# First stage of a four-layer graph network: node statistics ahead of the second mask tile; layer two's factor rows two sums sooner

## The reference, cut to what matters

```
h = relu(layernorm(x));  x = x + L0(h)   # project, layernorm, additive attention under adj, elu
h = relu(layernorm(x));  x = x + L1(h)   # 4-head attention under adj
h = relu(layernorm(x));  x = x + L2(h)   # relu(h W_self + mean over neighbours (h) W_neigh)
h = relu(layernorm(x));  x = x + L3(h)   # additive attention under adj
```

## Time and profile before

| what | us |
|---|---|
| median of 3 runs | 3532.34 (3532.33 to 3533.17) |
| the profiled execution | 3530.73 |
| its span (first to last instruction) | 3528.9 |
| mean granted TensorE clock of the span | 0.99 of full speed |

### The profile page before, as it was taken

The page is one execution under the profiler, slowest core; times in us unless marked ns, Lnnn a source line. Parts: engine busy times, 40 slices in busy tenths (PEclk is TensorE's granted clock), DMA queues, the critical chain, the costliest instruction groups (busy, mean ns, idle before and its releaser), DMA issues. The chain is left out here.

```text
span 3528.9 us, 58152 instructions
## 1 busy us (share of the span) xinstructions
PE 3409.4 (97%) x21140; PEld 1790.0 (51%) x21155; DVE 3066.7 (87%) x6862; ACT 1808.0 (51%) x4044; POOL 1830.4 (52%) x922
## 2 busy tenths in 40 slices
PE   6899998889999999999999999999998999899999
PEld 6799998431111111111111111111116999899999
DVE  8899997579999999999999999999977776677777
ACT  8633543766666666666666666666662554310010
POOL 7400101238888888888888888888870111000000
PEclk9999999999999999999999999999998999999999
DMA  8612121940011011101110111010003331312120
GB/s 301 220 69 91 55 91 54 291 161 10 25 30 30 8 27 30 30 6 29 30 30 5 30 30 30 6 30 30 6 7 108 120 120 73 121 67 91 55 91 25
DMA packets 78816, 234.62 MB, mean 66 GB/s; under 512 B 13504, under 2 KB 40768, under 8 KB 64448
## 3 DMA queue, kind: packets, MB, share of 16 engines
q1 hardware_dynamic: 77808, 230.56, 19.5%
q10 hardware_dynamic: 720, 0.33, 0.0%
HBM read 148.85 MB, written 81.99 MB: 65 GB/s over the span
## 5 line engine op out<-in xcount | busy, mean ns | idle before, releaser
L1828 POOL TENSOR_TENSOR a_w<-a_w,keep_mask_t 128x1024 f32<-128x1024 f32 x760 | 1608.0, 2141 | 306.1 <-ACT a_w L1813 306.1
L1813 ACT ACTIVATE a_w<-a_sc_ps 128x512 f32<-128x512 f32 x2048 | 1111.4, 595 | 705.1 <-PE a_sc_ps L1734 703.5
L1712 PE MATMUL a_o_ps<-a_w,a_v 128*33 128x512 f32 x4096 | 1079.1, 605 | 0.2
L1191 PE MATMUL g_acc<-g_hv,g_w 128*128 128x129 f32 x8192 | 923.2, 276 | 16.6 <-DVE g_w L1036 16.6
L1191 PEld LDWEIGHTS g_acc<-g_hv,g_w 128*128 128x128 f32 x8192 | 920.8, 193 | 17.9 <-ACT g_hv L1069 13.3
L1767 DVE CUSTOM_DVE_ANT_0 a_mx_ps<-a_mx_ps,a_mbias 128x512 f32<-128x512 f32 x1024 | 673.9, 718 | 39.5 <-PE a_mx_ps L1696 39.0
L1767 DVE CUSTOM_DVE_ANT_0 a_mx_ps<-a_mx_ps,em_mbias 128x512 f32<-128x512 f32 x968 | 636.5, 718 | 30.1 <-PE a_mx_ps L1696 29.8
L1734 PE MATMUL a_sc_ps<-a_qs,a_ks 97*128 97x512 f16 x2048 | 621.8, 385 | 0.5 <-ACT a_w L1813 0.2
L1780 DVE TENSOR_TENSOR a_w<-a_w,keep_mask_t 128x1024 f32<-128x1024 f32 x264 | 468.6, 1775 | 22.0 <-ACT a_w L1813 16.6
L1696 PEld LDWEIGHTS a_mx_ps<-a_ks,a_qs 32*128 32x128 f16 x1992 | 88.8, 91 | 784.9 <-DVE a_mx L1767 428.0
L1036 DVE SCALAR_TENSOR_TENSOR g_w<-f_row,keep_s,keep_mask_t 128x1024 f32<-128x1024 f32 x256 | 331.9, 1318 | 71.7 <-PE g_acc L1191 67.7
(11 more groups left out here) (313 smaller groups left out, 2383.2 us busy)
## 6 DMA issues: line engine op xcount, KB each, us to landing
p_adj_in<-in_adj SPq DMA_DIRECT2D x16, 1024.0 KB, 8.8
v<-p_v SPq DMA_DIRECT2D x32, 264.0 KB, 3.2
a_v<-v SPq DMA_DIRECT2D x16, 528.0 KB, 3.6
f_row<-u_rows SPq DMA_DIRECT2D x16, 512.0 KB, 5.9
g_x<-in_x SPq DMA_DIRECT2D x8, 1024.0 KB, 11.2
g_row<-u_rows SPq DMA_DIRECT2D x16, 512.0 KB, 8.1
x<-ho_o SPq DMA_DIRECT2D x16, 512.0 KB, 3.0
a_ks<-k_hi SPq DMA_DIRECT2D x64, 128.0 KB, 2.9
```

The source lines that it names most:

```text
L1191: mm = nc.tensor.matmul(tile(half, it), w[:, g % PB, it * P:(it + 1) * P], hv[:, k, jt, :], start=(jt == 0 and it % 3 == 0), stop=(jt == T ...
L1712: mm = nc.tensor.matmul(o_ps[2 * HD * a:2 * HD * a + HD + 1, c % 2, :], v[u][:, jt, a, :], w[:, g % PB, a, :], start=(jt == 0), stop=(jt = ...
L1813: nc.scalar.activation(w[:, g % PB, a], sc_ps[:, n % SB], ACT.Exp, scale=SCALE).then_inc(exp_done, 1)
L1828: nc.gpsimd.tensor_tensor(w[:, g % PB], w[:, g % PB], keep["mask_t"][:, jt, c * BANK:(c + 1) * BANK].unsqueeze(1).to_broadcast([P, 2, BANK ...
```

## The change

Three edits of order; no operation is added, removed or resized. In the first stage VectorE takes stats_x(b + 2) in front of mask(b, 1). In layer two's last round TensorE's tensor_rows comes after sum 7 instead of 9 and VectorE's vector_rows after sum 8 instead of 10. ScalarE's three exponentials come ahead of keep_h of the first two pieces instead of behind them.

```diff
--- before.py
+++ after.py
@@ -588,9 +588,9 @@
                 shift_of_x(b + 1)
                 if b > 0:
                     stats_h(b - 1, 1 - k)
-                mask(b, 1)
                 if b < B - 2:
                     stats_x(b + 2, k)
+                mask(b, 1)
                 if b > 0:
                     scores(b - 1, 1 - k)
 
@@ -2160,7 +2160,7 @@
                             fs.vector_diagonal(nc, dve, keep)
                         elif it == 5:
                             fs.vector_exponents(nc, dve, keep)
-                        elif it == 10:
+                        elif it == 8:
                             fs.vector_rows(nc, dve)
                 residual(b, k, 3)
                 stats3(b)
@@ -2269,10 +2269,11 @@
                     norm3(b - 1, 1 - k)
                     for q in range(CH):
                         keep_hT3(b - 1, q)
+                if last(b):
+                    fs.scalar(nc, act, keep)
+                if follows:
                     keep_h(b - 1, 0)
                     keep_h(b - 1, 1)
-                if last(b):
-                    fs.scalar(nc, act, keep)
                 for n in range(CH):
                     if more:
                         norm2(b + 1, 1 - k, n)
@@ -2383,7 +2384,7 @@
                         elif it == 4:
                             pe.wait_ge(consts_ready, 4)
                             fs.tensor_spread(nc, pe, keep)
-                        elif it == 9:
+                        elif it == 7:
                             fs.tensor_rows(nc, pe, keep)
                     if it in (4, 5) and follows:
                         turn3(b - 1, 2 * (it - 4))
```

## The result

The changed kernel takes 3543.7 us (median of 8 runs, 3540.39 to 3545.46), the kernel before 3532.9 us (8 runs beside it, 3529.83 to 3534.38). The ratio is 1.003, 95% interval 1.0021 to 1.0039: slower, by 0.21% to 0.39%. The forecast was 3536.6, with a range up to 3541.5.

A forecast was written before the change was run, and what follows sets the result against it. TensorE, busy 97% of the span, was taken as the bound, with VectorE, ScalarE and DMA nearly full in the first stage. First-stage reorder +4.3 us plus layer-two edits 0, on 3532.3, gave 3536.6 us; range 3531.0 to 3541.5.

The forecast's parts named there:

- The hole before the shift: First stage, VectorE's 0.87 us wait for GpSimd's power before the shift; forecast to close, at most 5.2 us over six shifts.
- both new waits: First stage: VectorE waiting for ScalarE's last feature copy before feature statistics, and for the nodes' load before node statistics.
- The first loop: First stage, second mask comparison through TensorE, ScalarE, feature and node statistics: 13.3 to 13.4 us, alone leaving 0.2 gain per turn.
- Edit 2: End of layer two: rows' transposition and copy two sums sooner, exponentials ahead; forecast 0 us, bounds −2.5 and +0.9.
- the reason given: Layer two's end: the rows' store stays behind the features' store in SyncE's queue, leaving at 3044.92 whichever way.
- The sum: First stage: four loops of 14.75 us from 40.94, then 6.89 us, put b = 6's mask tile 4.3 us later.
- the length L of the landing in the loop: First stage, landing of second adjacency tile, additive mask and nodes' load after the second comparison: 8.7 us by idle-queue rows.
- the end of the stage: From b = 6's mask tile on, order unchanged and no nodes loaded, so the stage ends the same 4.3 us later.
- The start: First stage, turn of b = 1: the first node statistics whose load can be late begin at 40.94, load about in time.
- The size of the loop: First stage, node statistics, second comparison, landing of three transfers and handover: 14.7 us, taken as 14.75 a turn.
- second reading: First stage: adjacency landings three turns apart give 14.75 us a turn, the cost of 4.74 MB for the slowest DMA engine.
- rival of a queue that does not drain: First stage: earlier transfers still delay the nodes' landing; loop from 15.44 us on, over 0.2% slower, 3544.8 at 16.8; chance 0.18.

The follow-up runs named there:

- e11: Kernel before with only the first-stage reorder, nodes' load cut to 64 KB from graph 3, 40 throw-away TensorE transpositions awaiting the second mask: 3536.1 us, ratio 1.0011.
- e2: Kernel before with only the layer-two edits (rows' transposition and copy sooner, exponentials ahead), first stage untouched: 3533.4 us, ratio 1.0002.
- e13: Kernel before with the nodes' statistics ahead of the second mask tile only in the turn of b = 5: 3535.0 us, ratio 1.0000.
- e12: Kernel before with only the second mask's additive form moved behind the nodes' statistics, and its store behind the nodes' load: 3531.2 us, ratio 0.9997.
- e14: Kernel before with the nodes' statistics ahead of the second mask tile in turns b = 0 to 4, not b = 5: 3541.7 us, ratio 1.0025.
- e1: Kernel before with only the first-stage reorder (nodes' statistics ahead of the second mask tile), layer two untouched: 3545.5 us, ratio 1.0035.
- e9: Kernel before with only the first-stage reorder, and the nodes' load cut from 1 MB to 64 KB from graph 3 on: 3535.0 us, ratio 1.0007.
- e8: Kernel before with only the first-stage reorder, and the mask's additive form stored behind the nodes' load: 3539.2 us, ratio 1.0018.
- e4: Kernel before with the first-stage reorder, nodes' load issued ahead of the second adjacency tile, 40 throw-away TensorE transpositions awaiting the second mask: 3538.6 us, ratio 1.0017.
- e5: Kernel before with only the first-stage reorder, plus 40 throw-away TensorE transpositions awaiting the second mask tile: 3546.1 us, ratio 1.0036.
- e10: Kernel before, order unchanged, with the nodes' load cut from 1 MB to 64 KB from graph 3 on: 3532.6 us, ratio 1.0002.

## Why the prediction was wrong

**Right.** The hole before the shift closed; both new waits stand where the prediction put them, and the one for the nodes' load decides. The first loop, 13.3 to 13.4 us, measured 13.3 to 13.5 in e11. Edit 2 is worth nothing that e2 could tell, for the reason given.

**Wrong.** The sum failed in two of its terms, the length L of the landing in the loop and the end of the stage, which it put at no cost; and its start was late. The loss of the stage in the trace is 145.26 − 132.82 = 12.4 us against 4.3 forecast. Term by term:

1. *The start.* "They would begin at 40.94, their load about in time." They began at 43.81, 2.9 us later. The feature statistics before them began at 38.39 instead of 37.12, after TensorE had stood 3.77 us and worked at the lower level (L711 behind it took 2.97 us for 12 products, where 1.61 is the time at the upper level), and the load was 1.49 us late. The first 1.3 us vary between executions: the feature statistics began at 37.12 to 38.42 in versions without the edit in that turn (before, e13, e12) and at 37.29 to 38.70 in versions with it (e14, e11). In e1 the load was in time and the node statistics began at 41.42, but the next loop then took 16.6 us.
2. *The size of the loop.* 15.4 us on average, (105.39 − 43.81) / 4, instead of 14.75: 4 × 0.65 = 2.6 us. The mis-sized term is L, 8.7 us by the rows of an idle queue, 9.4 to 9.7 in the four turns, 9.7 in the one above. The first transfer took 5.7 us, not 4.8; the other two took 4.0, where 3.9 was forecast. The prediction's second reading, that 4.74 MB cost the slowest DMA engine 14.75 us, gave nearly the same loop for a reason that does not hold: e12 moves the same bytes in 13.2 us a turn. The rule that the prediction weighed, the Trainium skill's fit of 2.0 us plus bytes over 436 GB/s (DMA: Bandwidth & Descriptors, "Anatomy of one DMA"), gives 8.0 and is further off.
3. *The end.* "From there no nodes are loaded and the order of the rest is unchanged, so the stage ends 4.3 us later." This step failed. The order was unchanged, but the state in which the lists enter it was not: 33.05 − 30.30 = 2.75 us. e13 and e14 show that it comes from the edited turn of b = 5, and the table of the tail, e9 and e11 above all, that most of it comes by TensorE's clock, which is at 0.50 behind the second mask tile of that turn. The prediction had no term for TensorE's waiting or its clock.

The three make 8.2 us, and with the 4.3 forecast 12.5, against the 12.4 us of the trace. In e1's trace the same three are 0.5, 3.6 and 2.1 us, 10.5 with the 4.3, against 143.18 − 132.82 = 10.4. The medians of the changed kernel and the one before lie 10.8 us apart. What edit 2 adds is less than e2 could tell.

The prediction's rival of a queue that does not drain gave the right side with a mechanism that was there at most in small part: in the kernel after the queue is dry or nearly so when the second tile is issued (the first tile's load landed from 0.8 us before that to 0.6 after), the nodes' load lands after 8.2 to 8.6 us and not 9.8, and the loop stays on average just under the 15.44 us that the prediction named as the point of decision. It was the start and the end that carried the time past 0.2%, so that the time came out on this rival's side is luck. TensorE's clock, which the prediction did not speak of, costs little while the load decides and most of the 2.75 us at the end.

## What to carry to other kernels

When an instruction is moved behind another one that waits for a transfer, look at what the moved one releases in the DMA queue: if the next turn's transfer is issued behind it, the move closes a loop, and its length is landing time plus work, not work alone. Size the landing from transfers issued in the same pattern, not from the best idle one. And when a turn's order changes, follow each engine's list out of the loop: a lag that the steady turns hide can come due in the first turn that is shorter. Where the new order makes TensorE stand, look at its granted clock behind the wait, in the last turn above all.

## What the runs showed of the hardware

- TensorE's granted clock was at its lower level (1.2 GHz) behind waits of 2.2 to 4.7 us in the turns of the changed kernel (turning a mask tile took 1.49 to 1.89 us instead of 1.07), and at the upper level (2.4 GHz) from 36 to 110 us of the kernel before, whose waits there were up to 1.4 us. The wait's length alone does not tell: e8 turned the last such tile in 1.07 us behind 2.99 us of waiting. 40 throw-away transpositions in the wait kept it at 1.00 in e4 and e11, and the stages ended 2.3 and 2.1 us earlier, which the medians could not show. In e5, where TensorE stood another 4.12 us behind them, it fell all the same.
- A 1 MB load took 4.8 us alone on an idle queue and 5.6 to 5.7 us in the turns of the changed kernel, also where the load before it had landed 0.8 us earlier. Behind a full queue it took up to 12.0 us. In the kernel before the landing times grew from turn to turn while VectorE waited for a DMA 0.25 us in all; with 1 MB less in a turn (e10) they did not grow.
